# Graph layer and experts kernel: the first layer's products moved from between the edge pairs to behind them

## The reference

```
x = x + gnn(layernorm(x))                 # 3125 nodes of 256 features, 50000 edges sorted by dst
x = x + moe(layernorm(x))                 # 16 experts, the best 2 for each row, then a layernorm

def gnn(h):
    ew  = clip(abs(edge_weight), 1e-6)
    deg = segment_sum(ew, dst) + 1
    dis = rsqrt(deg)
    for W, b, g, be in layer 1, layer 2:
        xw  = h @ W
        agg = segment_sum((dis[src] * ew * dis[dst])[:, None] * xw[src], dst)
        agg = agg + (dis * dis)[:, None] * xw
        h   = relu(layernorm(agg + b, g, be)) + h
    return h
```

## Time and profile before

| | us |
|---|---|
| Median of 3 runs | 1204.42 |
| Lowest and highest | 1200.83, 1205.97 |
| Span of the profiled execution | 1561.2 |
| TensorE busy in it | 1135.8 (73%) |
| VectorE busy | 731.4 (47%) |
| ScalarE busy | 414.0 (27%) |
| GpSimd busy | 601.3 (39%) |

### The profile page before, as it was taken

The page is one execution under the profiler, slowest core; times in us unless marked ns, Lnnn a source line. Parts: engine busy times, 40 slices in busy tenths (PEclk is TensorE's granted clock), DMA queues, the critical chain, the costliest instruction groups (busy, mean ns, idle before and its releaser), DMA issues. The chain is left out here.

```text
span 1561.2 us, 20045 instructions
## 1 busy us (share of the span) xinstructions
PE 1135.8 (73%) x6589; PEld 956.1 (61%) x6592; DVE 731.4 (47%) x2103; ACT 414.0 (27%) x933; POOL 601.3 (39%) x659
## 2 busy tenths in 40 slices
PE   3334434463423344999999998999999947999986
PEld 2222322342312233888888877888888837999984
DVE  7444533221111110444444443777777774554546
ACT  4302433322312100122222221222222212343446
POOL 6576656666666664000000000122222234555544
PEclk9999999966655556999999998999999978999998
DMA  7995000300000011333333303554544465222227
GB/s 244 372 397 230 1 1 0 125 3 1 1 1 1 1 48 43 127 127 126 127 126 128 126 1 132 195 193 160 173 149 160 159 190 171 71 72 73 72 59 247
DMA packets 80164, 180.80 MB, mean 116 GB/s; under 512 B 29042, under 2 KB 58364, under 8 KB 74044
## 3 DMA queue, kind: packets, MB, share of 16 engines
q1 hardware_dynamic: 48792, 151.67, 27.2%
q0 software_dynamic: 19776, 15.76, 3.7%
q10 hardware_dynamic: 11492, 12.07, 2.4%
HBM read 122.12 MB, written 57.33 MB: 115 GB/s over the span
## 5 line engine op out<-in xcount | busy, mean ns | idle before, releaser
L493 POOL DMA_INDIRECT weights_by_cell<-w_cell,cell x391 | 386.3, 988 | 211.9 <-issue 193.7
L1316 PE MATMUL ps<-x_rows,w 128*128 128x256 f32 x1250 | 290.9, 386 | 25.4 <-issue 19.6
L1316 PE MATMUL ps<-w 128*128 128x256 f32 x1300 | 298.9, 383 | 1.1 <-ACT w L967 1.1
L1316 PEld LDWEIGHTS ps<-x_rows,w 128*128 128x128 f32 x1250 | 237.9, 194 | 60.4 <-issue 23.9
L1316 PEld LDWEIGHTS ps<-w 128*128 128x128 f32 x1300 | 239.6, 190 | 31.3 <-ACT w L967 2.5
L552 POOL TENSOR_TENSOR x_rows<-hot,beta_b 128x256 f32<-128x256 f32 x25 | 18.1, 722 | 588.3 <-DVE hot L842 588.3
L1142 PEld LDWEIGHTS ps<-w,layer 128*128 128x128 bf16 x784 | 54.8, 113 | 124.9 <-issue 99.8
L1142 PE MATMUL ps<-w,layer 128*128 128x3 bf16 x784 | 54.3, 172 | 96.5 <-issue 85.7
L1149 PE MATMUL ps<-w,hot 128*128 128x75 bf16 x400 | 73.2, 316 | 69.6 <-issue 69.4
L1114 PE MATMUL ps<-key_part,pick 128*128 128x256 f16 x196 | 56.0, 377 | 87.1 <-issue 40.9
L698 DVE TENSOR_TENSOR layer<-ps,w 128x1024 bf16<-128x1024 f32 x70 | 84.8, 1218 | 71.9 <-remote 62.8
(11 more groups left out here) (246 smaller groups left out, 1525.2 us busy)
## 6 DMA issues: line engine op xcount, KB each, us to landing
w<-weights_by_cell SPq DMA_DIRECT2D x46, 1600.0 KB
weights_by_cell<-w SPq DMA_DIRECT2D x26, 1600.0 KB
w<-in_L_ffn_w_dram SPq DMA_DIRECT2D x32, 512.0 KB
weights_by_cell<-w_cell,cell POOLq DMA_INDIRECT x391
w<-in_x_dram ACTq DMA_DIRECT2D x1, 3072.0 KB
hot<-in_x_dram ACTq DMA_DIRECT2D x24, 128.0 KB
normalised_rows<-hot ACTq DMA_DIRECT2D x24, 128.0 KB, 6.8
out_dram<-w SPq DMA_DIRECT2D x24, 128.0 KB
```

What stands on the lines that cost most here:

```text
L493: pool.indirect_dma_start(adj[:, :], bass.IndirectOffsetOnAxis(ap=cell[0:m, c:c + 1].bitcast(U32), axis=0), w_cell[0:m, n, half * CH + j:h ...
L1316: mm = pe.matmul(bank(k % 2, 0, D), ring[:, place_of(k), s * P:(s + 1) * P], tab[q][:, s, :], start=(s == 0), stop=(s == NT - 1))
```

## The change

`T_TAB` is set to 196 (`SBS`), and `T_SCALE` and `T_TILE`, which are computed from it, become 248 and 252. The loops of TensorE and ScalarE run to `STEPS` = 302, and what belongs to the pairs is done only in steps below 196. So the turns, products and their copies stand in the steps 196 to 246, the scalings in 248 to 272, and the parts of matrix tile 0 in 252 to 300, all behind the last pair and ahead of matrix tile 1.

```diff
--- before.py
+++ after.py
@@ -56,9 +56,10 @@
 LOWS = -(-NT * P // 512)
 LOW_CHUNK = 8
 P_MEAN, P_SHIFT, P_DEG = 9, 22, HOT_LAST + 4
-T_APPLY, APPLY_STEP, T_TAB, TAB_STEP, T_DEG = 46, 4, 88, 2, 2 * P_DEG
+T_APPLY, APPLY_STEP, T_TAB, TAB_STEP, T_DEG = 46, 4, SBS, 2, 2 * P_DEG
 T_SCALE = max(2 * P_DEG + 6, T_TAB + TAB_STEP * NT + 2)
 T_TILE, TILE_STEP = T_SCALE + 4, 2
+STEPS = T_TILE + TILE_STEP * NT
 P_GUARD = T_APPLY // 2 + 2
 
 ACT_PAIRS = tuple(range(20, 54, 2)) + tuple(range(56, PAIRED - 1, 4))
@@ -984,10 +985,10 @@
                     act.activation(same[:, MRING, :, :, :].rearrange("p s h q -> p (s h q)"),
                                    key_gap.rearrange("p s h q -> p (s h q)"), ACT.Relu, bias=ones_f[:, 0:1], scale=-1.0).then_inc(same_by_act, 1)
 
-                for s in range(SBS):
+                for s in range(STEPS):
                     if s == 2 * ACT_PAIRS[0] - 5:
                         act_compare(ACT_PAIRS[0])
-                    if s % 2 == 1 and by_act(s // 2) and s // 2 != ACT_PAIRS[-1]:
+                    if s < SBS and s % 2 == 1 and by_act(s // 2) and s // 2 != ACT_PAIRS[-1]:
                         act_compare(ACT_PAIRS[ACT_PAIRS.index(s // 2) + 1])
                     if s == T_DEG:
                         act.wait_ge(deg_ready, 1)
@@ -1192,20 +1193,21 @@
                 for d in range(KBANKS):
                     key_rows(DVE_PAIRS[d], d, keyrow_ps)
                 pe.wait_ge(cols_ready, 1)
-                for s in range(SBS):
+                for s in range(STEPS):
                     for g in range(1, SG):
                         if s == 2 * part_pair(g, SIDE):
                             turn_part(g)
-                    if s % 2 == 0:
-                        next_key_rows(s // 2)
-                    weigh(s)
+                    if s < SBS:
+                        if s % 2 == 0:
+                            next_key_rows(s // 2)
+                        weigh(s)
                     if s == CH - 1:
                         limits()
-                    if s % 2:
+                    if s < SBS and s % 2:
                         for i in range(len(DEG_COLS)):
                             if hot_pair(i) == s // 2 - 1:
                                 degrees(i)
-                    if s % CH == CH - 1:
+                    if s < SBS and s % CH == CH - 1:
                         k = s // CH - LOW_CHUNK
                         if 0 <= k < LOWS:
                             pe.wait_ge(passed_ready, 1)
```

## The result

The changed kernel takes 1208.88 us (median of six runs, 1207.73 to 1210.77), the kernel before 1204.17 us beside it (six runs, 1200.83 to 1206.48): a ratio of 1.0043, with a 95% interval of 1.0026 to 1.0060. It is 4.7 us slower by the medians (5.2 by the ratio) where 12 were forecast. The interval lies wholly above 1, so the kernel is slower, but by about 0.4%: nearer to rival A's "hidden" (1204 us) than to the forecast's 1216.

The account below looks back on a forecast made before the run. GpSimd's placements and TensorE's matrix chain were taken to meet at the end of layer 1; 54 us put behind less 31 given back, less 10 slack, less 1, gave +12: 1216 us, range 1200 to 1240.

Parts of the forecast that it names:

- rival A: End of layer 1: placements end 20 us or more after the matrix chain and hide the growth; 1204 us, chance 0.25.
- Pairs: Pairs 44 to 97, freed of the moved work, give back 31 us; pair 97 ends at 194 us instead of 225.
- What is put behind: Behind pair 97: products at 1.6 us each, scalings and first tile, with slow start, add 54 us.
- Growth: TensorE's matrix chain up to the end of layer 1 grows by 54 - 31 = 23 us.
- Slack: At the end of layer 1, TensorE can be 10 us later before the time grows.
- The matrix sum: TensorE's pairs and 25 matrix tiles, 225 + 318, end layer 1 at 543 us in the kernel before.
- The placement sum: GpSimd's 391 scatters and waits take until 533 us; loading and the last two tiles end at 553 to 557.
- The sum's own anchor: End of layer 1 in a timed run, 1204.4 less 639.5 us of dense work: 564.9 us or some us earlier.
- less 1 for the load that is no longer waited for: SP's load of tile 3, no longer waited for after the change, takes 1 us off the forecast.
- B: Clock: pairs 44 to 97 run at half clock and give back 68 us against 57 put behind; 1193 us, chance 0.09.
- C: Interleaving was free: VectorE holds the pairs, which give back nothing; matrix chain grows by 54, 1248 us, chance 0.07.
- D: The edit doesn't do what it says to the step loops of TensorE and ScalarE; 1204 us, chance 0.01.

Follow-up runs that it names:

- the half change: Kernel before, with only the scalings and matrix tile 0 moved behind the last pair, turns and products left between the pairs; 1204.35 us, ratio 1.0003.
- the two-bank rows: Changed kernel, with the products behind the pairs going to two PSUM banks in turn; 1204.21 us, ratio 1.0011 to the kernel before.
- the two 16-row kernels: Kernel before and changed kernel, each scatter placing 16 of its 128 rows (7 of 8 edge weights left out); 1184.88 us (ratio 0.9845) and 1209.78 us (ratio 1.0045).
- the 54 products: Kernel before, with 54 extra unused products on TensorE ahead of matrix tile 1; 1208.40 us, ratio 1.0048.
- the disturbed execution: First profiled execution of the unchanged kernel before, the one the prediction read; span 1561.2 us, against 1204.4 us in timed runs.
- 27 products: Kernel before, with 27 extra unused products on TensorE ahead of matrix tile 1; 1203.53 us, ratio 1.0014.

## Why the prediction was right and wrong

*Pairs, right.* Tile 1 of the kernel before starts at 223.89 (225 forecast for the end of pair 97), the changed kernel's pairs end at 192.4 (194). They give back 31.5 us where 31 were summed; of the three parts of that sum only the last was seen by itself: in the half change the pairs' matmuls end at 217.04, 6.9 us sooner, where 8 were summed. In a stretch from 160 to 175 us VectorE, 7.28 us busy before, is busy for 15.00 of 15 us after: the pairs without products are held by its comparisons. The columns are as in the clock's row above; first the kernel before, then the changed one.

```profile
160.00:175.00 15.00, 13.40 (x130) 11.27 (x129) 7.28 (x11) 8.03 (x21) 11.61 (x12) 1.00 0.05 10
```

```profile
160.00:175.00 15.00, 12.17 (x169) 9.38 (x170) 15.00 (x22) 11.18 (x22) 11.63 (x12) 1.00 0.03 4
```

*What is put behind, right.* 192.4 to 248.03 is 55.6 us, where 54 stood. The products' pitch was 1.67 us, not 1.6, which makes up the difference. The first of them took 1.91 us (at 194.09), as long as the half-clock one of the earlier trace rows, and about the 1 us that was set aside; but the granted clock of 194 to 196 us reads 1.00, so that the cause of it is not shown. The split of a product into 0.89 and 0.14 us was not in the rows (the next matmul starts 0.87 us behind a product's start in the two-bank rows); their sum, 1.03, is.

*Growth, right.* 24.1 us in the traces, 24.9 between the two 16-row kernels, 23 in the sum.

*Slack, wrong, and this is the failing step.* "I take 10 us of slack" should have been some 18: 18.0 in the trace (559.19 less the 541.2 at which layer 1 would have ended without waits, 223.89 + 317.3), 18.8 by the 16-row kernel, 17.8 by the 54 products (23.6 less 5.8). With 18 in its place the sum is 23 - 18 = 5, and 4.7 were measured. The sign that was named for this step, a known delay of TensorE that costs all or none of its length, came true for the 11.9 us; the 23.6 us cost a part. The mechanism, two chains that meet at the end of layer 1, was right.

The 8 us are made up of three. The matrix sum was 2 us long (543 against 541.2). The placement sum was short: 553 to 557 against 559.2. And of the 10 to 14 us between the two sums I took the lowest.

The placement chain ended at 540.0 us, 7 later than the 533 of the sum. It was not the waits: between the first scatter and the last GpSimd was idle for 128 us (135.8 in the group of all 391, less the 8.0 ahead of the first), and the sum had 130 (390 times 0.305, and 10.9 for blanks), though the waits were for earlier placements and not for blanks. It was the scatters: 392.4 us for 391 of them, 1.003 each in the mean, where the sum had 0.97 from one row and 4 us for the early ones, 383. The page of the disturbed execution gave 386.3 for the same group. Of the 7 us some 4 reach the end of layer 1: the last but one load was issued 12.9 us ahead of the placements' end, not 10, TensorE started 5.8 us behind its issue (4 to 8 in the sum), and the two tiles took 26.3 us (25.7).

The lower end was taken with the argument that both sums leave out latencies and "the longer list more", meant for the matrix chain. It was the wrong way round: that chain ended sooner than its sum, the placement chain later. The sum's own anchor, layer 1 ending at 564.9 us in a timed run, stood above both sums and could have warned, but it was 5.7 us late itself: it gave 639.5 us to what follows layer 1, from the disturbed execution, where the second one had 641.9, and the timed run was 1.9 us longer than its span. The final "less 1 for the load that is no longer waited for" is shown by no run: the waits on loads are the slack itself, and taking them off once more counts them twice.

*Rivals.* A said that with the placement chain ending 20 us or more after the matrix chain nothing would be seen. Its mechanism is real, and its point was missed by little: 18 to 19 us of slack against the 20 that it named and the 24.1 of growth. That the time came out within 0.5% of before is thus mostly A's doing. With half the delay (27 products, half of the change, two banks) it is the whole answer. B, the clock, was not there: the granted clock of the kernel before's undisturbed edge stage is 1.00 from 20 to 175 us and 0.97 from 175 to 225, and the 0.55 of the earlier trace rows was the disturbed execution's. (B's own sum sets 57 us against the 68 where the forecast's had 54; with 54 its time is 1190, not 1193.) Where the clock did fall is behind the waits for loads in layer 1, which the prediction left out. C is out: the pairs gave back 31 us. D is out: tile 1 moved. The Trainium skill's "Perfetto Trace Analysis", "Optimization Strategy", says that interleaving regimes can help where the busiest engine changes over time. The traces agree in direction: the interleaving was worth 24 us of TensorE's chain. They add that some 18 of those paid for nothing, since TensorE was then waiting at the end of the layer.

*The span after* was forecast some 30 us over 1561, and was 1206.0. The stretched execution was one execution, not a property of profiling this kernel. Working around it by rebuilding the timed stage from undisturbed rows was sound for TensorE; for GpSimd it took a pitch from two rows, and the wrong name for a wait of nearly the right length.

## What to carry to other kernels

Where two chains meet, an edit on one is worth its size less the slack, so the slack deserves as careful a sum as the edit. It is a small difference of two large sums: 2 us of error in one and 4 in the other, of some 550, were half of it here. Take the time of an instruction that comes 391 times from the mean of all of them, not from one row: 0.03 us each were 13 us. A delay of known length on the suspected engine, and the other chain's work cut away, measure the slack from its two sides: delays of 11.9 and 23.6 us cost 1.6 and 5.8, and the cut gave 18.8, all from one slack of about 18 us. A piece of work that is cheaper when interleaved gains nothing as long as its engine waits later for something else.

## What was not expected of the hardware

- A scatter's time hardly goes with its rows: 1003 ns in the mean for 128 rows, 880 for 16, and the idle time, mostly put down to "issue", stays (135.8 and 131.8 us in all).
- The end of the placements differs from one execution to the next: the last load is issued at 538.0, 538.3, 539.8, 541.4, 541.7, 543.9 and 545.1 us in seven of these kernels, whose scatters are the same. So the start of layer 2 in a single trace is uncertain by some us: with the 27 products it was 556.24, sooner than the 559.19 of the kernel before, and only the medians compare the kernels. Whether the times of a kernel that is bound by it spread more for that reason is open: 16 runs of the kernel before lie within 7.2 us and 32 in another group within 9.4, but only four and seven of the 16-row kernels, within 2.5 and 3.7 us, stand beside them.
- A load of 384 KB landed in 3.7 us, one of 832 KB in 4.8, each with the second piece of its tile issued right behind it.
- After waits of 2.9 to 6.6 us for a load, TensorE's next 14 matmuls took 4.7 to 6.1 us instead of 3.29, with a granted clock down to 0.50 in them. After waits of 0.2 to 2.2 us they took 3.29, once 3.70 with the clock at 1.00. In the kernel before this cost nothing at the end of layer 1, since the next load was waited for all the same.
- One profiled execution was 357 us longer than every timed and every other profiled one of its kernel, in one stage, with idle time put down to "issue" and a granted clock of 0.55 in a stretch of it. Its idle rows were no guide to the stage; its TensorE rows at full clock were.
